# Expert outputs moved from VectorE to ScalarE, GpSimd and DMA, with VectorE's tap order regrouped

## What is computed

```python
x = x + conv(_ln_c(x))                    # norm over channels first
t = _to_tokens(x)
t = t + ffn(_ln_t(t))
x = _from_tokens(t, x)

# conv: four depthwise 3x3 convolutions (9 taps each)
value = _dwconv(x, w_v, b_v, 1)
query = _dwconv(x, w_q, b_q, 1).reshape(Bx * NH, HC, -1)
key = _dwconv(x, w_k, b_k, STRIDE).reshape(Bx * NH, HC, -1)
off = _dwconv(x, w_off1, b_off1, STRIDE)  # norm, gelu, 96 -> 2, tanh: positions
v_sampled = _grid_sample_bilinear(value, grid)
attn = jnp.einsum('bcm,bcn->bmn', query, key) * SCALE
out = jnp.einsum('bmn,bcn->bcm', attn, v_sampled)
y = jnp.einsum('bchw,oc->bohw', out.reshape(Bx, Cx, Hx, Wx), w_out)

# ffn: 4 experts 96 -> 384 -> 96, the top 2 gates kept and normalised
h = jax.nn.gelu(jnp.einsum('bsd,edh->ebsh', x, w1) + b1[:, None, None, :], approximate=False)
y = jnp.einsum('ebsh,ehd->ebsd', h, w2) + b2[:, None, None, :]
out = jnp.einsum('bse,ebsd->bsd', masked, y)
```

## Time and profile before

| | us |
|---|---|
| median of 3 runs (855.06 to 860.57) | 856.83 |
| profiled execution, its own time | 861.11 |
| its span, first to last instruction | 859.3 |
| PE, DVE, ACT, POOL busy in the span | 737.2, 617.6, 385.6, 328.9 |
| mean granted clock of PE, of full speed | 0.928 |

### The profile page before, as it was taken

How to read it: one execution, slowest core, us unless ns; L and a number is a source line. 1 busy time by engine, 2 the same in 40 slices (tenths; PEclk the granted TensorE clock), 3 DMA queues, 4 the chain that set the end, 5 groups by cost and what they waited for, 6 DMA issues and landing times.

```text
span 859.3 us, 9579 instructions
## 1 busy us (share of the span) xinstructions
PE 737.2 (86%) x3186; PEld 511.9 (60%) x3186; DVE 617.6 (72%) x1511; ACT 385.6 (45%) x722; POOL 328.9 (38%) x185
## 2 busy tenths in 40 slices
PE   4988998559992999899992999899993997999996
PEld 4656565336761666566761666566661665688885
DVE  5669827797859568798859468899984244477775
ACT  2323222524551316444551316544540136599995
POOL 4002600016659501256659502245586111234443
PEclk9997979679995999999996999999996799999999
DMA  7023100011420100114421100111421000211111
GB/s 177 1 56 127 43 0 1 0 36 56 151 72 18 35 17 25 43 41 113 153 68 26 41 3 25 51 37 52 153 79 43 17 25 17 67 41 57 65 56 33
DMA packets 20258, 45.58 MB, mean 53 GB/s; under 512 B 4977, under 2 KB 9841, under 8 KB 19921
## 3 DMA queue, kind: packets, MB, share of 16 engines
q1 hardware_dynamic: 12480, 30.18, 11.4%
q10 hardware_dynamic: 4656, 9.96, 3.6%
q0 software_dynamic: 3072, 4.82, 2.3%
HBM read 30.30 MB, written 14.65 MB: 52 GB/s over the span
## 4 chain that ended last, share of the span: by engine, by line
PE 59%; DVE 19%; POOL 11%; ACT 4%; issue 4%; DMA 1%; ACTq 1%; POOLq 0%; DVEq 0%
PE py L668 12%; POOL big L1309 11%; PE pd L626 7%; PE ph L525 5%; DVE val L1023 4%; PE pa L477 3%; PE ph L684 3%; PE ph L685 3%; PE ph L686 3%; PE pa L617 2%; PE pd L595 2%; PE py L721 2%; PE ph L706 2%; PE py L718 2%; PE ph L708 2%
## 5 line engine op out<-in xcount | busy, mean ns | idle before, releaser
L1317 POOL TENSOR_TENSOR xbuf<-xbuf,ye 96x448 f32<-96x448 f32 x112 | 206.6, 1845 | 434.7 <-DVE ye L1238 432.8
L668 PE MATMUL py<-hid,w 128*96 128x448 f32 x504 | 238.3, 554 | 16.6 <-DVE ye L1238 8.7
L899 ACT ACTIVATE hid<-ph,b 128x448 f32<-128x448 f32 x252 | 159.0, 634 | 163.7 <-PE ph L686 147.9
L684 PE MATMUL ph<-x_hi,w_hi 96*128 96x448 f32 x252 | 166.1, 659 | 0.0
L1309 POOL DMA_INDIRECT big<-value_table,rows x64 | 113.7, 1776 | 83.4 <-DMA value_table<-valT 64.2
L1238 DVE SCALAR_TENSOR_TENSOR ye<-py,b,gate_all 96x448 f32<-96x448 f32 x112 | 75.3, 675 | 64.9 <-PE py L668 57.3
L668 PEld LDWEIGHTS py<-hid,w 128*96 128x96 f32 x504 | 82.3, 167 | 38.6 <-ACT hid L899 14.2
L685 PE MATMUL ph<-x_lo,w_hi 96*128 96x448 f32 x252 | 94.4, 375 | 0.0
L686 PE MATMUL ph<-x_hi,w_lo 96*128 96x448 f32 x252 | 93.8, 372 | 0.0
L1023 DVE SCALAR_TENSOR_TENSOR val<-xpad,conv_w,val 128x784 f32<-128x784 f32 x80 | 91.2, 1188 | 0.3
L1280 DVE TENSOR_TENSOR hid_lo<-hid,hid_hi 128x448 fp32r<-128x448 f32 x84 | 59.7, 710 | 27.3 <-ACT hid L908 27.2
(11 more groups left out here) (152 smaller groups left out, 1118.2 us busy)
## 6 DMA issues: line engine op xcount, KB each, us to landing
gate_all<-gate_rows SPq DMA_DIRECT2D x56, 336.0 KB
value_table<-valT ACTq DMA_DIRECT2D x8, 1176.0 KB, 7.6
out<-xbuf SPq DMA_DIRECT2D x28, 168.0 KB, 2.1
xbuf<-in_x SPq DMA_DIRECT2D x3, 1176.0 KB, 8.3
big<-value_table,rows POOLq DMA_INDIRECT x64
xbuf<-in_x SPq DMA_DIRECT2D x2, 336.0 KB, 5.1
query<-in_w SPq DMA_DIRECT2D x1, 576.0 KB
w<-in_w SPq DMA_DIRECT2D x1, 576.0 KB
```

The lines of the kernel that those rows point to most:

```text
L668: nc.tensor.matmul(py[e % 2][0:C, 0:GPIX], w2[:, c, :], hid[:, k % 3, :], start=(j == 0), stop=(j == CPE - 1)).then_inc(hid_used, 1)
L684: nc.tensor.matmul(bank, w1_hi[:, cols], xh(b, g), start=True, stop=False)
L899: nc.scalar.activation(hid[:, k % 3, :], ph[k % 2][:, 0:GPIX], ACT.Gelu, bias=b1[:, k % NCH:k % NCH + 1]).then_inc(hid_act, 1)
L1317: ins = p.tensor_tensor(r, r, ye[0:C, e, :], ALU.add)
```

## The change

For images 0 to 2 an output no longer passes over DVE. ACT copies it from `py` with its bias into `ye` (`copy_output`), ahead of gelu 3n + 4 for output n, once output n - 4 has been added. POOL multiplies it by its gates in place and then issues a DMA that adds it to `xbuf`; each such DMA waits until the one before has landed. Gathers are dealt out: from output 6 on, POOL issues the two gathers of one tile between the product and the DMA of an output, for eight outputs. The last image's outputs are made on DVE and added on POOL as before. `FREE_OUTPUTS` and the two small memsets that stood for it are gone, and the semaphores `ye_ready` and `ye_summed` are replaced by `out_copied`, `out_gated`, `out_added`, `last_gated` and `last_added`.

On DVE `turn` and its account are gone. After the gates of image b come all nine value taps of image b + 1, with the raw positions behind tap 0; then, in the next round, positions, key taps, the norm of the image after, and all nine query taps.

```diff
-ROUND = [('valT', 28, 3, 19), ('xT', 33, 2, 0), ('keyT', 38, 0, 0), ('pad', 48, 3, 0), ('kv', 54, 0, 42), ('y', 57, 2, 3),
...
+GATHER_AT = 6
+LAST_GATHER_AT = 6
+DEALT = 1
+ROUND = [('valT', 24, 3), ('xT', 28, 3), ('keyT', 40, 2), ('pad', 49, 3), ('kv', 53, 2), ('y', 55, 2),
+         ('offT', 61, 0), ('x1c', 66, 3), ('exp', 75, 0), ('gateT', 78, 0), ('offc', 78, 0), ('offs', 81, 0),
+         ('tanh', 83, 0), ('end', 84, 0)]
+LAST_ROUND = [('valT', 18, 0), ('keyT', 34, 1), ('kv', 60, 0), ('y', 60, 0), ('x1c', 66, 3), ('exp', 70, 0),
+         ('gateT', 79, 0), ('end', 84, 0)]
...
+                def copy_output(n):
+
+                    g, e = n // EXPERTS, n % EXPERTS
+                    act.wait_ge(hid_used, b * CHUNKS + (n + 1) * CPE)
+                    added(act, b * OUTPUTS + n + 1 - EXPERTS)
+                    nc.scalar.activation(ye[0:C, e, :], py[e % 2][0:C, 0:GPIX], ACT.Identity, bias=b2[:, e:e + 1]).then_inc(out_copied, 1)
+
                 def gelus_to(end):
                     while done[0] < end:
                         k = done[0]
+                        if k >= CPE + 1 and k % CPE == 1:
+                            copy_output(k // CPE - 1)
...
-            def rest(b, with_head, turn):
-                for k in range(TAPS if first(b) else VALUE_AHEAD, TAPS):
-                    turn(2.7, "valT" if k == TAPS - 1 else None)
-                    value_tap(b, k)
-                    if k == VALUE_AHEAD:
-                        positions(b)
+            def rest(b, with_head):
+                if not first(b):
+                    positions(b)
                 for k in range(TAPS):
-                    turn(0.9)
                     key_tap(k)
-                turn(0.0, "keyT")
                 if with_head:
-                    turn(0.0, "xT")
-                    norm_x(b + 1, turn)
-                for k in range(0 if first(b) else QUERY_AHEAD, TAPS):
-                    turn(2.7)
+                    norm_x(b + 1)
+                for k in range(TAPS):
                     query_tap(b, k)
...
                 if with_head:
-                    for k in range(QUERY_AHEAD):
-                        turn(2.7)
-                        query_tap(b + 1, k)
-                    for k in range(VALUE_AHEAD):
-                        turn(2.7)
+                    for k in range(TAPS):
                         value_tap(b + 1, k)
                         if k == 0:
-                            raw_positions(b + 1, turn)
-                turn(0.0, "end")
+                            raw_positions(b + 1)
...
-            def sum_group(b, g):
-                i = b * NG + g
+            def add_group(b, g, beside):
+
                 r = x_of(b)[:, g * GPIX:(g + 1) * GPIX]
                 for e in range(EXPERTS):
-                    pool.wait_ge(ye_ready, FREE_OUTPUTS + i * EXPERTS + e + 1)
-                    ins = p.tensor_tensor(r, r, ye[0:C, e, :], ALU.add)
-                    ins.then_inc(ye_summed, 1)
...
+                    n = b * OUTPUTS + g * EXPERTS + e
+                    pool.wait_ge(out_copied, n + 1)
+                    if e % 2 == 0:
+                        pool.wait_ge(gate_in[e // 2], 16 * (b * NG + g + 1))
+                    p.tensor_tensor(ye[0:C, e, :], ye[0:C, e, :], gate_all[0:C, e, :], ALU.mult).then_inc(out_gated, 1)
+                    beside(e)
+                    pool.wait_ge(out_gated, n + 1)
+                    wait(pool, out_added, 16 * n)
+                    pool.dma_start(r, ye[0:C, e, :], accum_op=ALU.add).then_inc(out_added, 16)
```

More of the change, by code:

```diff
@@ L381, in wait, with gates_used, bank_free, added @@
                 eng.wait_ge(semaphore, value)
+        def gates_used(eng, number):
+            wait(eng, out_gated, min(number, DENSE))
+            wait(eng, last_gated, number - DENSE)
+        def bank_free(eng, number):
+            wait(eng, out_copied, min(number, DENSE))
+            wait(eng, last_gated, number - DENSE)
+        def added(eng, number):
+            wait(eng, out_added, 16 * min(number, DENSE))
+            wait(eng, last_added, number - DENSE)
         def slot(b, g):
@@ L947, in link, with statistics @@
                 need(step(ins))
-            def statistics(np_, nt, eps, with_mean, turn):
+            def statistics(np_, nt, eps, with_mean):
                 S = lambda k: st[0:np_, 0:nt, k]
@@ L1274, in last_experts @@
             def last_experts(b):
-                outputs_to = experts(b)
                 for k in range(CHUNKS):
@@ L1281, in last_experts @@
                     if k >= CPE + 1 and (k - 1) % CPE == 0:
[L1282 to L1286 removed]
+                        output(b, (k - 1) // CPE - 1)
+                output(b, OUTPUTS - 1)
             head(0)
[L1289 to L1296 removed]
+            for b in range(BATCH):
+                rest(b, b + 1 < BATCH)
             last_experts(BATCH - 1)
@@ L1302, in _, with gather @@
             p = nc.gpsimd
-            def gather(b):
-                pool.wait_ge(rows_ready, b + 1)
-                pool.wait_ge(table_out, 32 * (b + 1))
-                for k in range(NS):
+            def gather(b, tiles):
+                if 0 in tiles:
+                    pool.wait_ge(rows_ready, b + 1)
+                    pool.wait_ge(table_out, 32 * (b + 1))
+                for k in tiles:
                     for r in range(2):
@@ L1329, in _ @@
             pool.wait_ge(table_edge, 32)
-            gather(0)
-            for b in range(BATCH):
+            gather(0, range(NS))
+            for b in range(BATCH - 1):
+                start = GATHER_AT if b < BATCH - 2 else LAST_GATHER_AT
                 for g in range(NG):
-                    sum_group(b, g)
-                    if g == GATHER_AFTER and b < BATCH - 1:
-                        gather(b + 1)
+                    add_group(b, g, lambda e: gather(b + 1, range(NS)[max(0, DEALT * (g * EXPERTS + e - start)):max(0, DEALT * (g * EXPERTS + e - start + 1))]))
+            for g in range(NG):
+                add_last_group(BATCH - 1, g)
 def kernel(**inputs):
```

161 lines of the change are left out of this document (46 added, 115 removed).

## The result

The changed kernel takes 889.07 us (median of 4 runs, 883.84 to 891.17) against 855.94 us (4 runs of the kernel before beside it, 854.53 to 860.57): a ratio of 1.037, interval 1.031 to 1.043. The forecast was 907 us in a range of 858 to 970. Its sign and its mechanism held; its size, +50, was 17 us too large against the measured +33. The profiled execution took 891.17 us with a span of 889.4 us and a mean granted clock of 0.913 (859.3 us and 0.928 before).

What follows compares the result with a forecast made beforehand. The prediction took the time as PE's work (86% of the span) plus its idle time. Rounds 1 to 3 at +10, +16, +17 and clock +7 made +50: 861.1 profiled to 911, or 907 in the median's terms; range 858 to 970.

Steps and rivals of the forecast that it cites:

- The rows that decide: POOL stands still through an unbroken run of DVE taps, read from a gather issue of 21.55 us, 0.96 elsewhere.
- Part 1: Outputs leave DVE: 84 outputs, 57 us, removed; 84 ACT copies added at 0 us, hidden between gelus.
- Part 2: Sum by DMA on POOL: issue 1.3 plus landing 2.5, cycle 3.8 us, 5.0 with two gathers, against PE's 4.1.
- Rival B: The serial accumulation bounds all: landing in 4.0 us makes the cycle 5.3, 54 us, 961 us; chance 0.20.
- Part 3: DVE's new order: unbroken runs of 24 value taps (22.8 us), 24 key taps (8.2) and 24 query taps (22.8).
- 10 late: Round 2, value run: copy 2 of the new batch, due at 13.6 us, waits until output 26 is added at 23.7.
- 22 late: Round 2, query run: copy 13, due at 83.5 us, waits until output 9 is added at 105.7.
- 5 late: Round 2, key run: copy 4, due at 31.9 us, waits until output 0 is added at 36.9.
- 15: Round 1, value run: copy 4, due at 193 us, waits until 207.7, 15 us where 8.3 were.
- 21 late: Round 3, query run: copy 5, due at 41 us, waits until output 1 is added at 61.7.
- rival A: POOL gets in between single taps, losing at most one each time; 35 us faster, 826 or 822 us; chance 0.15.
- C: The four buffers cover more than counted: 15 us a round go, 862 us or so, no change; chance 0.07.

Runs made afterwards that it cites:

- e8: Changed kernel with one pause (VectorE waits for its own last tap) in each value and query run, at tap index 5: 846.0 us, ratio 0.986.
- e1: Changed kernel with VectorE waiting for its own last tap ahead of each value and query tap index from 2 on: 836.98 us, ratio 0.978.
- e3: Changed kernel with VectorE's old tap order put back, copies, products and accumulating DMAs kept: 863.7 us, no ratio formed.
- e4: Changed kernel with the sum as an addition on POOL in place of the accumulating DMA, new order kept: 885.36 us.
- e6: Changed kernel with VectorE waiting for its own last tap ahead of query tap indices from 2 on only: 860.06 us, ratio 1.010.
- e12: Changed kernel with VectorE waiting for its own last tap at tap indices 3, 5 and 7 of value and query runs: 831.13 us, ratio 0.973.
- e9: e1 with VectorE's old tap order, as in e3: 830.46 us, ratio 0.962.

## Why the prediction was right, and where it was off

**The rows that decide: right in five runs of the eight where POOL had work, wrong as a rule for all.** The earlier trace rows showed POOL held through an unbroken run, and the changed kernel shows it again (21.88, 22.98, 21.89 and 25.08 us to the end of the run, 12.20 through its second half). The forecast took every run to do so. The key runs of rounds 2 and 3 did not, that of round 1 met no POOL work, the value run of round 1 did not, and the query run of round 3 let one product in (at 634.74) and kept out the next, which came late, for its last 12.20 us. The Trainium skill, "SBUF — State Buffer", "Who interferes with whom", has the one that issued second wait for that one instruction. By that rule, the trace agrees in the value run of round 1 (products of 1.43 us between taps), and disagrees in the five above and in e8, where a product stood 10.54 us to the pause; there the measurement decides.

**Part 1, copies at no cost: not contradicted.** They take 628 ns, in gelus' gaps. Where POOL is let in (e1) no wait for a gelu is over 3.5 us; the 24.6 us of such waits that are left go with 30.9 us in which copies waited for a DMA. No run shows the copies' own cost apart.

**Part 2, POOL's cycle of 3.8 us and 5.0 with gathers: right.** After the value run of round 2 the accumulations were issued at 399.37 and 403.27, 3.9 us apart, the second after a wait of 1.95 us for the first, and the next ones likewise. With gathers they are 4.7 apart:

```profile
399.37 0.81 POOL L1259 DMA_DIRECT2D xbuf<-ye  x1 [0.29 <-POOL ye L1255]
...
403.27 0.81 POOL L1259 DMA_DIRECT2D xbuf<-ye  x1 [1.95 <-DMA xbuf<-ye]
...
478.34 0.98 POOL L1259 DMA_DIRECT2D xbuf<-ye  x1
...
483.01 0.99 POOL L1259 DMA_DIRECT2D xbuf<-ye  x1
```

The issue, 0.81 us, is cheaper than the forecast's 1.3, and the 3.1 us from there to the next issue are dearer than its 2.5. Missed was the landing beside the table's write: the accumulation issued at 634.20 let the next one go only at 647.01, shown above with its wait of 10.84 us. Rival B, 961 us, needed a cycle over 4.1 everywhere.

**Part 3 and the sum, run by run.** "10 late" at the value runs of rounds 2 and 3 was 9.54 in both. "22 late" at the query run was 23.64 in round 1 and 21.37 in round 2. "5 late" at every key run was 0. "15" at the value run of round 1 was 6.2, by another way, the transposes' wait for a run that POOL had made longer. "21 late" in round 3 was 10.48. These last three are the step that failed, for one reason: it took each unbroken run to keep POOL out from its first instruction to its last. At the key runs even that would not have cost much: where other kernels show such a stand (7.4 to 8.4 us in e3, e4 and e6), no copy waited over 4 us behind it.

**Rounds and clock.** Forecast +10, +16, +17 and +7 for the clock on top; measured, clock included, +5.2, +20.9 and +3.9. The clock's own part is read from PE's busy time for the same matmuls, +8.1, against the 7 of the forecast. In round 2 it shows by the granted clock of the round (the column behind the five engines' busy times). First the changed kernel, then the kernel before:

```profile
374.00:585.00 211.00, 172.09 (x735) 113.22 (x735) 138.25 (x335) 97.50 (x185) 117.54 (x72) 0.90 0.34 75
```

```profile
369.00:559.00 190.00, 165.78 (x737) 110.83 (x737) 147.65 (x363) 82.49 (x157) 91.76 (x44) 0.96 0.19 58
```

Round 3 was off by a second term besides the query run. Its kv ended 125.4 us after the offsets' product, 17.8 later than before (27 forecast); but from there to the round's end it took 66.1 us in place of 80.0, 13.9 less, where the forecast took off 8.2 for six chunks and 1.9 for a wait. The 11.7 us wait before kv was gone, and with it the lower clock behind it (0.93 over those 80.0 us, 0.97 over the 66.1). The forecast had this in rival A ("some 6 of clock behind it") and left it out of its own sum.

**The rivals.** A, openings between single taps, 822 us, did not happen by itself, but e1 and e12 made it happen, at 837 and 831: its working was close, and it told what the change could have given. C had runs let in upon once on the way. That happened in four of the nine (the value run of round 1, the key runs of rounds 2 and 3, the start of the query run of round 3), not in the others.

## What to carry to other kernels

Before moving a step to GpSimd, look for the longest unbroken run of two-input VectorE instructions, count GpSimd as absent for all of it, and divide by the pace of whoever waits: 22 us at 4.1 us an output asks for more than five buffers, and there were four. Then look where GpSimd stands before the run: if it comes there late, as here from its wait for the table, the buffers are in use and cover almost nothing. Where buffers can't be had, break the run: one pause in its middle was worth 43 us, three 58 and seven 52 (the last two not told apart by their rounds), each a wait of VectorE on itself (a one-element memset ahead of each tap index did as well as the wait there). And price an edit in the kernel as it will be: against the addition the DMA sum gained nothing or 25 us, the old order 25 or 6.5, the pause 52 or nothing, by what bounded the kernel around them.

## What the runs showed of the hardware

- Whether an unbroken run of two-input VectorE instructions keeps GpSimd out was not constant. Products that came 0.01 us before a tap (377.19 and 588.69) stood 21.9 us; one that came 0.10 us before one (187.48) was through in 1.43, and all later ones of that run too, but one that came 0.11 us before one (452.82) stood 22.98. So the moment of arrival alone does not tell them apart, and what decides it stays open.
- Runs of small taps (128 x 196) were no exception: they let products in (1.43 us, changed kernel) or kept one out (8.42 us over 23 of them in e3, 6.85 over 18 in e1).
- Each POOL step that gets in holds VectorE: 24 value taps took 30.45 us with seven products begun in them and 22.78 without.
- The issue of a plain accumulating DMA on GpSimd was never held: 0.807 to 1.001 us over all 84, while a gather's issue took up to 25.08.
- An accumulating DMA of 168 KB within SBUF let the next one go 3.9 us after its issue began (399.37 to 403.27), and 12.8 us after it beside the table's write (634.20 to 647.01).
- Not tried: the old order with three pauses (e9 and e12 are the two best, 830.5 and 831.1 us, 24 to 25 us under the kernel before and not told apart), more than four buffers, and gathers dealt out later or otherwise, so that POOL does not stand at the table's write ahead of the query run.
